# A two-layer decoder on one core: first four context pairs fetched during the retention, and both transposed contexts of odd pairs fetched instead of one

## The reference, cut to what matters

```python
q = query @ Wq + bq                      # (32, 56, 128)
k = ctx @ Wk + bk                        # (32, 1500, 128)
v = ctx @ Wv + bv
out = softmax(q @ k.T / sqrt(128)) @ v   # residual added by the caller
```

## Time and profile before

| | |
|---|---|
| runs, us | 1640.2, 1640.3, 1646.28 (median 1640.3) |
| profiled execution, us | 1648.14, with a span of 1646.3 |
| retention, us of the span | 16 to 119 |
| context attention, first block | 119.6 to 138.5 |
| context attention, loop | 139.5 to 294.8 |
| mean granted TensorE clock | 0.969 |

### The profile page before, as it was taken

The page is one execution under the profiler, slowest core; times in us unless marked ns, Lnnn a source line. Parts: engine busy times, 40 slices in busy tenths (PEclk is TensorE's granted clock), DMA queues, the critical chain, the costliest instruction groups (busy, mean ns, idle before and its releaser), DMA issues. The chain is left out here.

```text
span 1646.3 us, 45184 instructions
## 1 busy us (share of the span) xinstructions
PE 1531.0 (93%) x16354; PEld 1189.8 (72%) x16354; DVE 1122.2 (68%) x1760; ACT 896.3 (54%) x1419; POOL 699.9 (43%) x754
## 2 busy tenths in 40 slices
PE   7988999889999877789999999999999999889998
PEld 3544666689999655467777777777777777578887
DVE  2643555668787459467777777777777777267777
ACT  4454333432223337446666666666666666467776
POOL 0210000477787446543444433444433443256665
PEclk8988999999999889899999999999999999989999
DMA  2008995131110000366655556655556654202211
GB/s 76 2 20 207 260 262 151 39 107 62 64 41 22 1 1 2 100 156 152 151 130 131 131 131 149 149 132 130 130 131 149 149 133 113 56 23 79 69 66 45
DMA packets 53547, 168.83 MB, mean 103 GB/s; under 512 B 12640, under 2 KB 25280, under 8 KB 53472
## 3 DMA queue, kind: packets, MB, share of 16 engines
q1 hardware_dynamic: 51312, 156.30, 37.9%
q10 hardware_dynamic: 2160, 11.52, 2.2%
HBM read 90.27 MB, written 1.03 MB: 55 GB/s over the span
## 5 line engine op out<-in xcount | busy, mean ns | idle before, releaser
L1871 DVE TENSOR_REDUCE hat_tops<-banks 128x1 f32<-128x500 f32 x672 | 442.0, 677 | 151.5 <-PE banks L1620 151.5
L1744 ACT ACTIVATE hat_pb<-banks 125x896 f32<-125x896 f32 x384 | 340.2, 916 | 224.7 <-PE banks L1639 220.9
L1620 PE MATMUL banks<-hat_kh,hat_qm 128*128 128x500 f32 x672 | 299.6, 463 | 3.5 <-DVE hat_tops L1871 3.3
L1639 PEld LDWEIGHTS banks<-hat_q,hat_k 128*125 128x125 f32 x1536 | 219.5, 188 | 72.8 <-ACT hat_pb L1744 31.7
L1639 PE MATMUL banks<-hat_q,hat_k 128*125 128x224 f32 x1536 | 250.4, 286 | 14.3 <-ACT hat_pb L1744 9.1
L1813 POOL CAST hat_kh<-hat_kf 128x500 fp32r<-128x500 f32 x96 | 58.3, 607 | 405.6 <-ACT hat_kf L1757 391.3
L1630 PE MATMUL banks<-hat_pb,hat_vs 125*27 125x168 f32 (+1 forms) x6144 | 166.9, 261 | 0.1
L1630 PEld LDWEIGHTS banks<-hat_pb,hat_vs 125*27 125x27 f32 (+1 forms) x6144 | 132.3, 98 | 43.8 <-issue 24.3
L1198 ACT ACTIVATE ffn_rg<-banks 128x448 f32<-128x448 f32 x128 | 69.7, 544 | 164.7 <-PE banks L1132 164.6
L1620 PEld LDWEIGHTS banks<-hat_kh,hat_qm 128*128 128x128 f32 x672 | 128.2, 192 | 40.9 <-DVE hat_tops L1871 25.4
L2113 DVE TENSOR_TENSOR moe_hl<-moe_hf,moe_hh 128x448 fp32r<-128x448 f32 x128 | 108.5, 887 | 42.2 <-POOL moe_hh L2005 41.6
(11 more groups left out here) (280 smaller groups left out, 3067.1 us busy)
## 6 DMA issues: line engine op xcount, KB each, us to landing
hat_k<-hat_kh SPq DMA_DIRECT2D x256, 187.5 KB, 4.8
hat_ct<-ctxT SPq DMA_DIRECT2D x32, 750.0 KB, 6.1
hat_k<-hat_kl SPq DMA_DIRECT2D x128, 187.5 KB, 4.5
ctx_cx<-ctx SPq DMA_DIRECT2D x32, 672.0 KB
ctx_cd<-ctxT ACTq DMA_DIRECT2D x15, 750.0 KB, 4.7
ffn_cb<-expert_weights SPq DMA_DIRECT2D x8, 896.0 KB, 4.3
moe_cb<-expert_weights SPq DMA_DIRECT2D x8, 896.0 KB, 6.2
moe_raw<-Mw SPq DMA_DIRECT2D x18, 256.0 KB, 2.9
```

What stands on the lines that cost most here:

```text
L1620: peak_out.inc(nc.tensor.matmul(g.bank(PK + m % 2)[:, 0:SB], qm[u][:].rearrange("p h i -> p (h i)")[:, r * 128:r * 128 + 128], kh[u][:, c ...
L1639: mm = nc.tensor.matmul(g.bank(2 * (t % 2) + j // 2)[0:SW, (j % 2) * QW:(j % 2 + 1) * QW], k3[u][:, j, t * SW:(t + 1) * SW], q3[u][:, j, : ...
L1744: exped.inc(nc.scalar.activation(pb[t % 6][:].rearrange("p (n i) -> p n i", n=2), g.ps[0:SW, 2 * (t % 2):2 * (t % 2) + 2, 0:2 * QW], ACT.E ...
L1871: peaked.inc(v.tensor_reduce(tops[:, r, n:n + 1], g.bank(PK + m % 2)[:, 0:SB], AX_X, ALU.max))
```

## The change

The first loads move from the first block of the context attention to SP's part of the first block of the retention, behind its 25 weight transfers. For that, `cx`, `cd` and their semaphores are allocated ahead of the retention, by a new class. In the loop, even pairs stay as they are. For odd pairs ACT also issues a transfer of the transposed second context into a new buffer `ce`, and PE waits for it; the 12 transposes and the three ACT copies are left out. `e` counts the even pairs for the semaphores of the transposes.

```diff
@@ def retention(g, ahead)
                     if name not in EARLY:
                         sp.dma_start(g.w[name][:], g.d[name]).then_inc(g.late_in, 16)
+                ahead.first_loads(sp)
...
+class ContextAhead:
+    def __init__(self, g, ctx):
...
+        self.cx = [[sb(f"cx{w}{k}", [SW, ST, D]) for k in range(2)] for w in range(4)]
+        self.cd = [sb(f"cd{u}", [128, 3, SB]) for u in range(2)]
+        self.loaded = [g.semaphore(f"ctx_loaded{w}") for w in range(4)]
+        self.straight = [g.semaphore(f"ctx_straight{u}") for u in range(2)]
+
+    def load(self, sp, p, w):
+        for k in range(2):
+            for a, b in ((0, 112), (112, SW)):
+                source = self.g.d["ctx"][p * 2 + k].rearrange("(p t) d -> p t d", t=ST)
+                sp.dma_start(self.cx[w][k][a:b], source[a:b]).then_inc(self.loaded[w], 16)
+
+    def first_loads(self, sp):
+        self.load(sp, 0, 0)
+        sp.dma_start(self.cd[0][:], self.g.d["ctxT"][0].rearrange("p (n s) -> p n s", n=3)).then_inc(self.straight[0], 16)
+        for p in range(1, 4):
+            self.load(sp, p, p)
+
+def retention_and_context(g):
+    with ExitStack() as ctx:
+        ahead = ContextAhead(g, ctx)
+        retention(g, ahead)
+        context_attention(g, ahead)
...
@@ def context_attention(g, ahead)
-        ct = sb("ct", [128, 3, SB])
+        ct, ce = sb("ct", [128, 3, SB]), sb("ce", [128, 3, SB])
+        second_straight = sem("second_straight")
...
         with nc.Block() as block:
-            block.sync(first_loads)
-
...
@@ PE
-                def scores(p, u, parts):
+                def scores(e, u, parts):
                     for n in parts:
-                        c_copied.wait(pe, p, n + 1)
+                        if u == 0:
+                            c_copied.wait(pe, e, n + 1)
                         for k in range(2):
-                            mm = nc.tensor.matmul(..., cd[u][:, n, :] if k == 0 else ct[:, n, :],
+                            mm = nc.tensor.matmul(..., (cd[u], ce if u else ct)[k][:, n, :],
...
+                    e = f * 2 + w // 2
                     pe.wait_ge(loaded[w], 64 * f + 64)
-                    turn_context(p, w, (0, 1))
+                    if u == 0:
+                        turn_context(e, w, (0, 1))
                     if third:
                         weigh(p - 2, (w + 2) % 4)
-                    turn_context(p, w, (2,))
+                    if u == 0:
+                        turn_context(e, w, (2,))
...
                     pe.wait_ge(straight[u], 32 * f + 16 * (w // 2) + 16)
+                    if u == 1:
+                        pe.wait_ge(second_straight, 32 * f + 16 * (w // 2) + 16)
...
@@ ACT
                 def straighten(p, u):
                     scored.wait(act, p - 2)
                     act.dma_start(cd[u][:], g.d["ctxT"][p * 2].rearrange(...)).then_inc(straight[u], 16)
+                    if u == 1:
+                        act.dma_start(ce[:], g.d["ctxT"][p * 2 + 1].rearrange(...)).then_inc(second_straight, 16)
...
                 def slot(p, w, f):
                     scored.wait(act, p - 1)
-                    copies(p, (0, 1))
+                    if w % 2 == 0:
+                        copies(f * 2 + w // 2, (0, 1))
...
-                    copies(p, (2,))
+                    if w % 2 == 0:
+                        copies(f * 2 + w // 2, (2,))
```

More of the change, by code:

```diff
@@ L334, in _, with retention @@
             dve.wait_ge(normed, CH)
-def retention(g):
+def retention(g, ahead):
     nc, c_ = g.nc, g.c
@@ L624, in _, with context_attention @@
                 dve.wait_ge(normed2, CH)
-def context_attention(g):
+class ContextAhead:
+    def __init__(self, g, ctx):
+        sb = lambda n, s: ctx.enter_context(g.nc.sbuf_tensor(f"ctx_{n}", s, F32))
+        self.g = g
+        self.cx = [[sb(f"cx{w}{k}", [SW, ST, D]) for k in range(2)] for w in range(4)]
[17 more added lines that the diff above has]
+        context_attention(g, ahead)
+def context_attention(g, ahead):
     nc, c_ = g.nc, g.c
@@ L637, in context_attention @@
         zt = g.xn
-        cx = [[sb(f"cx{w}{k}", [SW, ST, D]) for k in range(2)] for w in range(4)]
-        cd = [sb(f"cd{u}", [128, 3, SB]) for u in range(2)]
-        ct = sb("ct", [128, 3, SB])
+        cx, cd, loaded, straight = ahead.cx, ahead.cd, ahead.loaded, ahead.straight
+        ct, ce = sb("ct", [128, 3, SB]), sb("ce", [128, 3, SB])
+        second_straight = sem("second_straight")
         part = [sb(f"part{u}", [128, 2, 2 * L]) for u in range(2)]
@@ L644, in context_attention @@
         z = sb("z", [128, 128])
-        loaded, straight = [sem(f"loaded{w}") for w in range(4)], [sem(f"straight{u}") for u in range(2)]
         q_out, q_done, k_out, k_done = sem("q_out"), sem("q_done"), sem("k_out"), sem("k_done")
[L648 to L658, removed]
         norm = Normal(g, ctx, "n2", [(g.w["Wo"][:], g.xn)])
         with nc.Block() as block:
-            block.sync(first_loads)
             @block.tensor
@@ L703, in slot @@
                         pved.wait(sp, p - 4)
-                        load(sp, p, w)
+                        ahead.load(sp, p, w)
                 four_ends(sp, slot)
@@ L723, in turn_weights, with turn_context @@
                         p_turned.inc(mm)
-                def turn_context(p, w, parts):
+                def turn_context(e, w, parts):
                     for n in parts:
-                        c_copied.wait(pe, *((p, n - 1) if n >= 2 else (p - 1, 2 + n)))
+                        c_copied.wait(pe, *((e, n - 1) if n >= 2 else (e - 1, 2 + n)))
                         for t in range(4):
@@ L731, in turn_context @@
                         turned.inc(mm)
-                def scores(p, u, parts):
+                def scores(e, u, parts):
                     for n in parts:
-                        c_copied.wait(pe, p, n + 1)
+                        if u == 0:
+                            c_copied.wait(pe, e, n + 1)
                         for k in range(2):
-                            mm = nc.tensor.matmul(g.bank(4 + n)[64 * k:64 * k + L, 0:SB], part[u][:, 1, k * L:k * L + L], cd[u][:, n, :] if k == 0 else ct[:, n, :],
+                            mm = nc.tensor.matmul(g.bank(4 + n)[64 * k:64 * k + L, 0:SB], part[u][:, 1, k * L:k * L + L], (cd[u], ce if u else ct)[k][:, n, :],
                                                   start=True, stop=True)
@@ L766, in slot @@
                                          start=True, stop=True)
-                    scores(p, u, (0,))
+                    scores(e, u, (0,))
                     if second:
@@ L771, in slot @@
                         turn_sums(p - 2)
-                    scored.inc(scores(p, u, (1, 2)))
+                    scored.inc(scores(e, u, (1, 2)))
                 four_ends(pe, slot)
@@ L787, in straighten @@
                     act.dma_start(cd[u][:], g.d["ctxT"][p * 2].rearrange("p (n s) -> p n s", n=3)).then_inc(straight[u], 16)
+                    if u == 1:
+                        act.dma_start(ce[:], g.d["ctxT"][p * 2 + 1].rearrange("p (n s) -> p n s", n=3)).then_inc(second_straight, 16)
                 def exponentials(p, u):
@@ L794, in exponentials, with copies @@
                                                    bias=small[:, u, 2:3], scale=scale, accum_out=small[:, u, 3:4]))
-                def copies(p, parts):
+                def copies(e, parts):
                     for n in parts:
-                        turned.wait(act, p, n + 1)
+                        turned.wait(act, e, n + 1)
                         c_copied.inc(nc.scalar.copy(ct[:, n, :], g.bank(n % 2)[:, 0:SB]))
@@ L2229, in decoder @@
         g.ct_dram = nc.dram_tensor("expert_weights", [E, NT], F32).ap()
-        stages = [(begin,), (retention,), (context_attention,),
+        stages = [(begin,), (retention_and_context,),
                   (experts0,), (causal_attention,),
```

## The result

The changed kernel is slower: 1658.84 us median (1656.81 to 1660.65, four executions) against 1641.35 of the kernel before in the same series; ratio 1.0079 with a 95% interval from 1.0057 to 1.0102, some 13 us. (The two medians differ by more, 17.5 us. In a later series of eight executions of the changed kernel the ratio was 1.0086.) I had forecast 1644.2, no change, and given a slowing by more than 0.5% a chance of 0.29. The interval lies wholly in that case, the second rival. On the base of the prediction, 1640.3, the ratio is 1653 us, in the upper end of its range (1634 to 1656); the median itself is above it. That 1653 lies in the range is owed to the second rival, whose number set its upper part; the forecast's own case ended at 1648.

The account below looks back on a forecast made before the run. PE bound the kernel, with the DMA engines close to their limit in the context loop. Terms -1.3 (odd slots), -3.0 (slot 1) and +8.2 (added transfers) sum to +3.9 us: 1644.2 against the median of 1640.3, range 1634 to 1656.

Parts of the forecast that it names:

- the second rival: Context loop becomes a DMA stream at 259 GB/s, 20.8 us per pair of slots; total 1651, chance 0.27.
- the forecast's own case: DMA-bound context loop at 18.4 to 20.3 us per pair of slots; total 1637 to 1648, chance 0.43.
- The chain: Odd slots: maximum, small steps and exponentials beside PE get no shorter, so PE gains only 0.19 us each, 1.3 us together.
- Slot 1 and the early loads: Context loop, slot 1: pair 1's transposed contexts arrive early, removing a DMA wait; 3.0 us gained, partly at low clock.
- The loads in the retention: Retention's first block: SP's 17 new issues end at 38.5, before the block's end at 47, and cost nothing.
- ACT's second issue, taken at 0: Even slots: ACT's second transfer issue fits before the exponentials, costing 0; bound of 3 us if held up.
- The price of a pair of slots: Context loop: DMA time for 5.376 MB per two slots, between 18.4 and 20.8 us, against PE's 17.57.
- I take the middle, 19.6 us: DMA time per pair of slots taken between both bounds, 274 GB/s; 8.2 us lost over six pairs after the lead.
- The low bound: DMA time per pair of slots from the old loop's packet times: 18.4 us, losing 1.0 us.
- The lead of 4 us: Context loop: transfers land some 4 us before they are needed, and this is eaten before late transfers cost time.
- The clock as a surcharge of "up to 5 us more": Context loop, within the second rival: waits may also lower PE's clock, adding up to 5 us.
- The limit of about 358 GB/s per core: Skill's HBM limit: the loop's 306 GB/s would be had, nothing lost, sum -4.3 us; the prediction sided against it.

Follow-up runs that it names:

- the run with 128 partitions: Changed kernel with each plain context fetched in one transfer of 128 partitions (three following rows unread) instead of 112 and 13; ratio 0.9977 to the kernel before.
- the two kernels with the old loop: Kernel before with early loads and its loop unchanged, ratio 0.9991; the same with plain contexts fetched in transfers of 128 partitions, ratio 0.9992.
- the idle transposes: Changed kernel in which PE also makes the 12 transposes in odd slots, into banks nobody reads; ratio 1.0068 to the kernel before, changed kernel 1.0086 beside it.

## Why the prediction was right or wrong

*The chain*: right. Odd slots gain next to nothing from the 1.39 us; the run with 128 partitions shows 1.0 us for seven of them, against 1.3 forecast.

*Slot 1 and the early loads*: right in the trace, 3.1 us against 3.0, with the low clock in the first part of the stretch as assumed (products of 1.04 us until 152, 0.58 from 154 on). Seven other traces with early loads have the same slot 1, 10.1 to 10.2 us; one has 11.49. In the total of the two kernels with the old loop the 3 us did not come out of the noise. The loads in the retention were free, and ended at 38.6 us as worked out (38.5).

*ACT's second issue, taken at 0*: held. The changed kernel's list of waits from 155 to 300 has ACT's exponentials behind DVE 14 times and behind an issue once, for 0.6 us.

*The price of a pair of slots*: this step failed, as the term "I take the middle, 19.6 us". The slots took 21.05. The DMA engines' part of that is 20.4 (5.376 MB at the measured 263 GB/s); the other 0.6 us I put down to the stops and the low clock, which is not shown by a run. Lost were 16.1 us where the sum had 8.2. Both bounds had been laid at 18.4 and 20.8, and the row that was nearest to the new state was the saturated one, 259 GB/s, 20.8 us. The low bound was wrong in itself, since it took the packets' times of a loop in which the engines rest for 0.09 of the time. These times did not hold in the changed kernel (DMA queues from 160 to 290):

```profile
q1 hardware_dynamic: 3696, 18.43, 57.0%
q10 hardware_dynamic: 2723, 14.50, 36.6%
```

A plain packet takes 0.57 x 16 x 130 / 3696 = 0.321 us, against 0.299 by the earlier trace rows, and a transposed one 0.280 against 0.257. By these a pair of slots costs 19.9 us and not 18.4. The run with `ce` fetched once shows from the other side that there was hardly any room before.

*The lead of 4 us*: it held for slots 2 and 3 and was gone by slot 5, as one would expect at 20 to 21 us per pair.

*The clock as a surcharge of "up to 5 us more"*: too small by the rows. Half of the 16.5 us by which the four long slots grew is work that took longer at 1.2 GHz. How much of that the kernel would win back with the clock at 1.00 stays open, since the transfers would be late all the same; the idle transposes won 3 us, within the noise. In the forecast's own case I had left the clock out, with the argument that a stop of 1.52 us leaves it at 1.00. That row is of the weight loads; PE itself stood for 1.28 us there. The runs bear the argument out for such a stop alone. It does not hold for two stops close together, nor for a single one of 2.7 us.

*The limit of about 358 GB/s per core*, for which the prediction cites the Trainium skill, "DMA: Bandwidth & Descriptors", section Specifications: the trace does not agree that 306 GB/s would be had. The saturated loop with 112 partitions stayed at 263 GB/s. Into 128 partitions two transfers at a time ran near the limit, at 338 to 351, and the 128-partition loop has slices of 2.6 us with 414 to 433 GB/s, so in this program, on one core alone, it wasn't a ceiling either. What decided was which partitions the transfers cover.

## What to carry to other kernels

Price a transfer by a row of its own kind, with the same number of partitions and in a stretch that is as saturated as the new one will be. Where no such row exists, time it in an empty queue. A DMA share a little below 1 does not say that more would fit. Before PE's work is traded for bytes, follow the chain beside that work, since 1.39 us removed in front of a wait were worth 0.14. If a tile has a few partitions less than 128, fetching the missing rows along and ignoring them can be far cheaper than cutting it in two, as 112 and 13.

## What was unexpected in the hardware

Loads of rows of 6000 or 6144 bytes, two transfers at a time in an empty queue, ran at 351 GB/s into 128 partitions, 197 to 202 into 112, 155 into 64 and 129 into 125, and cutting 112+13 further made it slower (178 to 199 against 223). At 125 partitions the DMA share was 0.31, five sixteenths; the Trainium skill, "DMA: Bandwidth & Descriptors", section "Why a DMA increments its semaphore by 16 and not by 1", says that the number of engines is the largest one up to 16 that divides the partitions, which is 5 for 125, and the row agrees. By that rule 112 has all 16 engines, and the share (0.77 to 0.97) agrees too, yet the rate is only six tenths of that of 128. Why stays open; no run tried it.

Late transfers came in bursts: the changed kernel's loop had four long slots in one trace and five in the other, in other places but for slots 5 and 10, and the rest within 0.4 us of their normal length, though the mean demand never changed.
